# A graph network's head: indices computed ahead of the wait for the floor fill, boundary rows gathered between the scatters

## The reference

```python
src = jnp.concatenate([_s, _d, _loop]); dst = jnp.concatenate([_d, _s, _loop])   # 212,500 edges
_o = jnp.argsort(dst, stable=True); src = src[_o]; dst = dst[_o]                 # sorted by dst
...
def _L0_gnn_ref(x, edge_index, W1, b1, W2, b2):
    x_i = x[dst]
    x_j = x[src]
    edge_features = jnp.concatenate([x_i, x_j - x_i], axis=-1)
    h = jax.nn.relu(edge_features @ W1 + b1)
    edge_messages = h @ W2 + b2
    out = jax.ops.segment_max(edge_messages, dst, num_segments=x.shape[0])
    return jnp.where(jnp.isfinite(out), out, jnp.zeros_like(out))
def _L1_gnn_ref(x, edge_index, edge_attr, u, batch, W1a, ...):
    out = jnp.concatenate([x[row], edge_attr], axis=1)
    out = _mlp(out, W1a, b1a, g1a, be1a, W2a, b2a)      # linear, batch norm, relu, linear
    out = jax.ops.segment_sum(out, col, num_segments=x.shape[0])
    out = jnp.concatenate([x, out], axis=1)
    return _mlp(out, W1b, b1b, g1b, be1b, W2b, b2b)
...
h = jnp.maximum(_layernorm(x, axis=-1), 0.0)
x = x + _L0_gnn_ref(h, edge_index, L0_gnn_W1, L0_gnn_b1, L0_gnn_W2, L0_gnn_b2)
h = jnp.maximum(_layernorm(x, axis=-1), 0.0)
x = x + _L1_gnn_ref(h, edge_index, edge_attr_64, ...)
```

## Time and profile before

| what | value |
|---|---|
| timed, median of 3 runs | 5362.03 us (5359.89 to 5370.35) |
| profiled execution, span from first to last instruction | 5881.6 us |
| POOL busy | 3763.8 us (64%) |
| DVE busy | 2407.0 us (41%) |
| PE busy | 2132.4 us (36%) |
| ACT busy | 1147.2 us (20%) |
| stage 1 | 0 to 343 us |
| stage 2 | 343 to 2677 us |
| stage 3 | 2677 to 2853 us |
| stage 4 | 2853 to 5228 us |
| stages 5 and 6 | 5228 to 5882 us |

### The profile page before, as it was taken

One profiled execution on the slowest core, in us unless ns is written; L12 is line 12 of the kernel. 1 busy time (PEld: TensorE's weight loads), 2 busy tenths in 40 slices (PEclk: granted clock), 3 DMA queues, 4 the chain that ended last, 5 costly groups with the idle time before them and its releaser, 6 DMA issues. The chain is left out here.

```text
span 5881.6 us, 27215 instructions
## 1 busy us (share of the span) xinstructions
PE 2132.4 (36%) x6371; PEld 1168.9 (20%) x6371; DVE 2407.0 (41%) x3005; ACT 1147.2 (20%) x1966; POOL 3763.8 (64%) x3772
## 2 busy tenths in 40 slices
PE   2012222222222222220144344444444344457776
PEld 1001101111010111100022222222222222235555
DVE  5324444444444444446322222222222222259995
ACT  6100000000000000000111111111111111148884
POOL 5667777777777777776666666666666666621112
PEclk9986666566666656665566665666666666668887
DMA  9523323233333333331233333333333333359993
GB/s 352 174 61 82 79 72 80 72 80 75 77 79 73 79 72 80 73 75 38 49 99 88 98 99 88 88 98 88 98 88 99 98 88 98 91 215 423 424 421 124
DMA packets 352728, 710.63 MB, mean 121 GB/s; under 512 B 147428, under 2 KB 219082, under 8 KB 305875
## 3 DMA queue, kind: packets, MB, share of 16 engines
q1 hardware_dynamic: 206708, 573.33, 27.7%
q0 software_dynamic: 119328, 128.91, 11.0%
q10 hardware_dynamic: 26534, 6.66, 0.5%
HBM read 363.85 MB, written 344.74 MB: 120 GB/s over the span
## 5 line engine op out<-in xcount | busy, mean ns | idle before, releaser
L721 POOL DMA_INDIRECT hid<-send_table,node_sums x1664 | 1748.7, 1051 | 554.5 <-issue 554.5
L981 POOL DMA_INDIRECT pairs<-norm_table,node_sums x1664 | 1570.5, 944 | 793.6 <-issue 476.0
L735 PE MATMUL ps_msg<-hidden,w_quarters 128*128 128x512 f32 x832 | 612.3, 904 | 1858.5 <-ACT hidden L748 1171.7
L1001 PE MATMUL ps_hid<-pairs_t,w1a 128*128 128x512 f32 x832 | 684.4, 917 | 1211.5 <-ACT pairs_t L1033 620.3
L1085 DVE TENSOR_SCALAR hid<-ps_hid,vec 128x512 f32<-128x512 f32 x416 | 311.3, 748 | 1743.5 <-DMA mid_row<-recv_table,mid_idx 972.6
L735 PEld LDWEIGHTS ps_msg<-hidden,w_quarters 128*128 128x128 f32 x832 | 237.2, 300 | 2233.0 <-ACT hidden L748 1231.7
L775 DVE STREAM_TRANSPOSE send_t<-hid 128x1024 f32<-128x1024 f32 x104 | 131.0, 1259 | 1274.6 <-DMA hid<-send_table,node_sums 1274.6
L1033 ACT COPY pairs_t<-ps_pairs 128x512 f32<-128x512 f32 x416 | 244.1, 587 | 1721.2 <-remote 1369.2
L748 ACT ACTIVATE hidden<-joined 128x1024 f32<-128x1024 f32 x104 | 109.9, 1056 | 2358.2 <-DMA entries<-dst_groups,group_idx 1236.4
L1218 DVE TENSOR_TENSOR_SCAN total<-ps_mask,total,hid 128x1024 f32<-128x1024 f32 x208 | 488.7, 2350 | 48.7 <-PE ps_mask L1168 26.1
L1001 PEld LDWEIGHTS ps_hid<-pairs_t,w1a 128*128 128x128 f32 x832 | 180.6, 270 | 1296.5 <-ACT pairs_t L1033 661.1
(11 more groups left out here) (163 smaller groups left out, 1949.7 us busy)
## 6 DMA issues: line engine op xcount, KB each, us to landing
hid_edges<-hid SPq DMA_DIRECT2D x104, 1024.0 KB
hid<-hid_edges SPq DMA_DIRECT2D x104, 1024.0 KB
hid_edges<-rows SPq DMA_DIRECT2D x104, 1024.0 KB
recv_edges<-node_sums SPq DMA_DIRECT2D x52, 1024.0 KB
hid<-recv_edges SPq DMA_DIRECT2D x416, 128.0 KB
max_edges<-hid SPq DMA_DIRECT2D x416, 128.0 KB
edge_in<-in_edge_attr_dram SPq DMA_DIRECT2D x415, 128.0 KB
hid<-send_table,node_sums POOLq DMA_INDIRECT x1664
```

What stands on the lines that cost most here:

```text
L721: pool.indirect_dma_start(out=send_in[:, s, j * C:(j + 1) * C], out_offset=None, in_=send_table, in_offset=bass.IndirectOffsetOnAxis(ap=sr ...
L735: mm = nc.tensor.matmul(ps_msg[k % M][:, d, :], w2_quarters[:, b, d, :], hidden[:, s % 2, b, :], start=b == 0, stop=b == BANDS - 1)
L981: pool.indirect_dma_start(out=pairs[:, s, j, 0:C], out_offset=None, in_=norm_table, in_offset=bass.IndirectOffsetOnAxis(ap=src_cols[:, k / ...
L1001: nc.tensor.matmul(ps_hid[s % 2][:, :], w1a[:, :], pairs_t[:, s % 2, :], start=True, stop=True).then_inc(multiplied, 1)
```

## The change

Two things are written in another order, and the boundary rows take another way.

- VectorE's wait for the floor fill, the memset and `mbig` move from before the index chain to behind it, directly ahead of the transposes. Nothing in them is changed.
- POOL's gather of the boundary rows moves from behind the 100 scatters to before pair 44 (`MID_AT`), that is before scatter 88, with its two waits. SP writes the three rows to a DRAM tensor of their own (`mid_rows`) as soon as they are there, and waits for the scatters last.
- Stage 2 begins on SP with six transfers (three quarters, two bands of 32 channels) from `mid_rows` into the last column of `filled[:, 1]`, one element per partition. This column is the start state of the first scan. They wait for VectorE's memsets of it, and VectorE waits for them (`mids_set`) before its first step.

```diff

--- before.py
+++ after.py
@@ -147,6 +147,7 @@
     recv_edges = dram("recv_edges", (EP, C))
     max_edges = dram("max_edges", (EP, C))
     norm_table = dram("norm_table", (NP, C))
+    mid_rows = dram("mid_rows", (3, C))
     CHUNK = 4 * BLK
     assert CHUNK == CO
     hid_edges = dram("hid_edges", (NCO, P, CHUNK))
@@ -305,6 +306,7 @@
 
             pool_passed, dve_passed = sem("pool_passed1"), sem("dve_passed1")
             FILLS = EP * C // (P * CO)
+            MID_AT = NI // 2 - 6
             PIECE_BITS = (P * CO // C).bit_length() - 1
             assert P * CO // C == 1 << PIECE_BITS and NI % 2 == 0
             filled, fill_known = sem("filled"), sem("fill_known")
@@ -359,10 +361,10 @@
                 sp.dma_start(same_max.rearrange("(p c) -> p c", c=CO), mbig[:, :]).then_inc(masks_out, 16)
 
                 sp.wait_ge(mid_gathered, 16)
-                sp.wait_ge(scattered, 16 * NI)
-                sp.dma_start(recv_edges.rearrange("(q e) c -> q e c", q=4)[1:4, 0, :], mid_row[0:3, :]).then_inc(mid_out, 16)
+                sp.dma_start(mid_rows, mid_row[0:3, :]).then_inc(mid_out, 16)
                 sp.wait_ge(mid_out, 16)
                 sp.wait_ge(masks_out, 32)
+                sp.wait_ge(scattered, 16 * NI)
 
             @block.gpsimd
             def _(pool):
@@ -395,6 +397,11 @@
                 pool.wait_ge(fill_known, 1)
                 pool.wait_ge(recv_made, NSTEP)
                 for h in range(NI // 2):
+                    if h == MID_AT:
+                        pool.wait_ge(tables_out, 32)
+                        pool.wait_ge(mid_in, 64)
+                        pool.indirect_dma_start(out=mid_row[:, :], out_offset=None, in_=recv_table,
+                                                in_offset=bass.IndirectOffsetOnAxis(ap=mid_idx[:, 0:1], axis=0)).then_inc(mid_gathered, 16)
                     needed = pool.value_load(fills_needed[0:1, h:h + 1], min_val=1, max_val=FILLS)
                     pool.wait_ge(filled, needed)
                     pool.sem_inc(pool_passed, 1)
@@ -402,10 +409,6 @@
                         pool.indirect_dma_start(out=recv_edges, out_offset=bass.IndirectOffsetOnAxis(ap=start_idx[:, i:i + 1], axis=0),
                                                 in_=recv_sb[:, i, :], in_offset=None,
                                                 bounds_check=EP - 1, oob_is_err=False).then_inc(scattered, 16)
-                pool.wait_ge(tables_out, 32)
-                pool.wait_ge(mid_in, 64)
-                pool.indirect_dma_start(out=mid_row[:, :], out_offset=None, in_=recv_table,
-                                        in_offset=bass.IndirectOffsetOnAxis(ap=mid_idx[:, 0:1], axis=0)).then_inc(mid_gathered, 16)
 
             @block.tensor
             def _(pe):
@@ -581,12 +584,6 @@
                 nc.vector.tensor_tensor(w_ab[:, 0:C], w_ab[:, 0:C], w_ab[:, C:2 * C], ALU.subtract).then_inc(w_made, 1)
 
                 pipeline(dve, SSTEP, SLOTS, [(0, find_group), (3, find_start), (1, norm), (4, add_bias)])
-                for s in range(2):
-                    dve.wait_ge(floor_out[s], 16 * (FILLS // 2))
-                nc.vector.memset(quarter_rows[3 * W:P, E - (P - 1) * IPP:IPP], 0).then_inc(src_padded, 1)
-                dve.wait_ge(masks_made, 1)
-                nc.vector.tensor_scalar(mbig[:, :], m01[:, :], 2 * BIG, -BIG, ALU.mult, ALU.add).then_inc(masks_made, 1)
-
                 def to_row(result, edges, add):
 
                     once.link(nc.vector.tensor_copy(edge_i[:, :], edges))
@@ -631,6 +628,11 @@
                                                              in1=spans[:, :], op0=ALU.is_equal, op1=ALU.mult))
                     once.link(nc.vector.tensor_scalar(spans_mid[:, b, :], spans[:, :], BIG, -BIG, ALU.mult, ALU.add))
 
+                for s in range(2):
+                    dve.wait_ge(floor_out[s], 16 * (FILLS // 2))
+                nc.vector.memset(quarter_rows[3 * W:P, E - (P - 1) * IPP:IPP], 0).then_inc(src_padded, 1)
+                dve.wait_ge(masks_made, 1)
+                nc.vector.tensor_scalar(mbig[:, :], m01[:, :], 2 * BIG, -BIG, ALU.mult, ALU.add).then_inc(masks_made, 1)
                 dve.wait_ge(src_in, 16 * 11)
                 nc.vector.transpose(src_quarters.rearrange("p b a -> p (b a)").bitcast(F32), quarter_rows[:, :].bitcast(F32)).then_inc(src_made, 1)
                 for k in range(KH):
@@ -668,7 +670,7 @@
             (recv_turned, send_turned, fill_done, join_done, hidden_done, msg_done, max_done, rows_made, w2_clear, w2_in) = (
                 sem(n) for n in ("recv_turned", "send_turned", "fill_done", "join_done", "hidden_done", "msg_done", "max_done",
                                  "rows_made", "w2_clear", "w2_in"))
-            fill_start = sem("fill_start")
+            fill_start, mids_set = sem("fill_start"), sem("mids_set")
             block = s2.enter_context(nc.Block())
 
             def by_row(tile):
@@ -684,6 +686,12 @@
                 recv_v = recv_edges.rearrange("(q k p j) c -> q k p (j c)", q=4, p=W, j=JQ)
                 max_v = max_edges.rearrange("(q k p j) c -> q k p (j c)", q=4, p=W, j=JQ)
                 mask_v = same_max.rearrange("(q k c) -> q k c", q=4, c=BLK)
+                sp.wait_ge(fill_start, 2 * BANDS)
+                with nc.allow_non_contiguous_dma(reason="one element per partition"):
+                    for q in range(1, 4):
+                        for b in range(BANDS):
+                            sp.dma_start(filled[q * W:(q + 1) * W, 1, b, BLK - 1:BLK],
+                                         mid_rows[q - 1:q, b * W:(b + 1) * W].rearrange("a p -> p a")).then_inc(mids_set, 16)
                 sp.wait_ge(w2_clear, 1)
                 for q in range(4):
                     for b in range(BANDS):
@@ -755,6 +763,7 @@
                     nc.vector.memset(filled[:, 1, b, BLK - 1:BLK], -BIG).then_inc(fill_start, 1)
                     nc.vector.memset(maxima[:, 1, b, BLK - 1:BLK], -BIG).then_inc(fill_start, 1)
                 dve.wait_ge(fill_start, 2 * BANDS)
+                dve.wait_ge(mids_set, 16 * 3 * BANDS)
 
                 def fill(r, s):
                     k = r * U + s
```

## The result

The changed kernel takes **5334.12 us** (median of 4 runs, 5332.78 to 5335.07); the kernel before, on the same chip, takes 5360.96 (4 runs, 5359.58 to 5370.35). The ratio is 0.9948 with a 95% interval of 0.9935 to 0.9962: 26.8 us or 0.52% faster.

A forecast was written before the change was run, and what follows sets the result against it. POOL's indirect gathers were taken to bound the long stages 2 and 4. Terms: −1.2 (chain starts earlier) + 0.2 (POOL) + 0 (boundary rows) + 0 (added transfers) = −1.0 us, giving 5361.0 us, range 5346 to 5369.

The forecast's parts named there:

- the price of the wait: Stage 1, VectorE before the index chain: fill complete 1.4 us before VectorE needs it, so the wait costs nothing.
- Rival A: Head: in timed runs VectorE is ahead of the floor fill, old kernel loses 13.6 us there; 5347.4 us, chance 0.18.
- The two moved instructions: Head: memset and mbig leave the index chain's path, 1.2 us gained, less 0.2 for POOL running beside them.
- The boundary rows: End of stage 1: SyncE about 1.2 us earlier in the barrier, but POOL's drain closes the stage; gain 0.
- Rival B: End of stage 1: POOL's drain is short without the profiler, so SyncE's 1.2 us count too; 5359.8 us, chance 0.10.
- The added transfers: Start of stage 2: six transfers take 2.5 us of SyncE's issue, but POOL does not wait; cost 0.
- Source loads and the tables: Stage 1: later source loads have 80 us of cover, the boundary gather's tables 57 us; cost 0.
- rival C: Start of stage 2: new transfers bring POOL's slow pace on at once, ten steps by 2.4 us; 5385 us, chance 0.06.
- D: Head: POOL blocked for both moved instructions (1.16 us), or the receive table holds the scatters; stays 5362.0 us, chance 0.06.

The follow-up runs named there:

- new profile of before: The kernel before, unchanged, profiled a second time: 5360.36 us, with a span of 5358.6.
- the two runs that part them from the wait: Whole change with only the wait put back ahead of the index chain: 5359.26 us; whole change with memset and mbig back there, without the wait: 5334.08 us.
- the memset behind them: The whole change with a 128x128 memset on POOL behind the last scatter: 5334.99 us, ratio 0.995 to the kernel before.
- faster version: The whole change with the first 20 columns' indices computed inside the norm loop and scattered early, boundary gather before pair 47: 5319.12 us, ratio 0.9921.

## Why the prediction was wrong, and where it was right

**The step that failed: the price of the wait.** The prediction read a margin of 1.4 us for the fill out of the first profile, and said that in this execution the wait costs nothing. Of that execution this was true. The failure is in the step that carried it over to the timed runs: "So I take the head to be about as long in the timed runs". The timed median stood 519.6 us below that span. The prediction placed 491 of it in POOL's gathers, which was right (496 by the new profile), and treated the other 29 as too little to matter. But a surplus of 28 us in VectorE's head is all that it takes to turn a wait of 26.3 us into one of zero. The new profile of before shows it: receive table at 157.85 in place of 186.03, the fill at about 184 in both. The runs put that wait, 26.3 us long, in the place of the zero: the wait's move alone gave the whole gain, and the wait put back took it away.

**The sum as it was.** First scatter: 191.46 − 164.56 = 26.9 us earlier. Start of stage 2: 331.44 − 305.05 = 26.4 us earlier. Timed: 26.8. Of this the two moved instructions are 0.75 to 0.83 by the two runs that part them from the wait, and the wait is the rest, about 25.6.

**Rival A was right in kind and too small.** Its mechanism is the one that decided: VectorE is ahead of the fill in the timed runs. Its size came from spreading the surplus evenly, 8.8% of 169 us or 15 us, and the surplus was not even: 28 us. With 28 in place of 15, a number that only the later profile gives, its own working gives 28 − 1.4 = 26.6 us for the wait and 1.0 for the rest, 5334.4 us, against 5334.12 measured. Its chance, 0.18, was set too low by an argument that doesn't hold: "DVE's stalls fall together with POOL's gathers, which are real work". The gathers stand beside the same VectorE steps in the new profiles, without these stalls: of the ten L211 in the new profile of before, nine run wholly inside a gather, and none has idle time ahead of it. So the stalls were part of the stretched execution. A surplus that shows beside real work is not thereby real itself.

The Trainium skill (SBUF — State Buffer, section "SBUF: two separate sides") gives the lock of the shared ports a condition that the prediction left out: a VectorE operation with two SBUF inputs takes it only against a GpSimd operation that reads SBUF. The prediction let the stall of the earlier trace rows agree with the lock. The new profile of before takes that agreement away: the same operation on two inputs starts at 54.54, in the midst of the gather of 54.30 to 55.25, and does not wait. So these gathers don't block it. What stalled it in the first profile stays open.

**The two moved instructions.** Predicted 1.2 less 0.2 for POOL, 1.0 in all. In the changed kernel the scatter beside `mbig` (189.44) lasts 1.16 us in place of 0.98, which is the 0.2. For the whole the traces give 0.75 and 0.83. That bears the term out to within the spread from profile to profile: the receive table alone was done at times up to 1.1 us apart in the nine later ones. No timing shows it.

**The boundary rows.** Predicted 0, since POOL's drain closes the stage. Borne out: the boundary rows alone measure 1.0001, with SyncE 2.4 us earlier in the barrier (1.2 were predicted) and the drain's end unmoved. In the changed kernel the drain ends 9.1 us after POOL's last transfer, as in the earlier trace rows (9.2). The reason given, that the drain belongs to POOL's transfers, is not shown: with the memset behind them, its end kept its distance from the memset. The forecast needs only that POOL's last instruction stays where it was, and it did (321.18 against 321.25). Rival B, a drain that is short in timed runs, would have made this kernel some 2.4 us faster; the timing alone doesn't exclude that, since its interval reaches down to 0.9992, 4.3 us. What speaks against B is that the later profiles, whose spans agree with the timed runs, have the drain's end 9.1 to 9.2 us behind POOL's last instruction.

**The added transfers.** Predicted 2.5 us on SyncE and 0 on the path. They took 2.63 us, and the first join still waited 5.20 us for gathers. With five times as many, the weights 11.2 us later and the first join 5.8 us later, the time was the same. Borne out.

**Source loads and the tables.** The transposes end at 241.6 + 3.4 = 245.0, and POOL scatters until 294.9: about 50 us of cover where 80 were predicted, since the scatters themselves moved. The tables of the boundary gather are out by 262.2 and the gather comes at 278.41: 16 us of cover where 57 were predicted. POOL waited for neither (0.30 us ahead of the gather, as ahead of any scatter), as predicted, but both margins shrink by the gain itself: the earlier the scatters start, the less of them is left. The faster version puts the gather ahead of pair 47 for this reason.

**Rivals C and D.** Stage 2 keeps 20.0 us a step, in the changed kernel and in the new profile of before; no later profile has the slow pace of 22.4 us, and so rival C loses its ground. What tipped the pace in the first profile stays open. The two halves of D fall with the first scatter 26.9 us earlier and with the one scatter that grew by 0.2 us and not by 1.16.

**What is given back.** The fill ends 4.4 us later when scatters run beside its last parts (memset at 188.55 against 184.16; 190.25 in the faster version). It costs nothing here, since what waits for it has the cover named above: about 50 us for the source indices, 16 us for the tables, whose transfers wait for the fill too.

## What to carry to other kernels

Before a margin of one or two microseconds is read out of a profile, compare its span with the timed median. Here they differed by a tenth, and the difference wasn't spread evenly. A first sum found nearly all of it, and the little that was left was enough to hide the wait. In such a case every wait whose two sides are of different kinds, instructions on one and transfers on the other, should be priced with the whole unplaced rest on either side, or the profile taken again.

Work that needs nothing from a wait belongs ahead of it even where the wait looks empty in one profile. What then comes later is the work that stood behind the wait, so look up its cover first (here 50 us were left). With that cover the move is an insurance against the runs in which the wait is not empty.

After a wait is gone, look at once at the idle time ahead of the same instruction: here POOL's 15.05 us were still there, and a second cut of the same chain brought 15 us more.

## What the runs showed of the hardware

One profiled execution of the kernel before had a span of 5881.6 us, where the next one had 5358.6 and the timed runs about 5361. Of the surplus 226 us lay in stage 2's gathers (2303.2 against 2077.3 for the same 1664, of which 178 us in the gathers' own busy time, 1748.7 against 1570.5) and 270 us in stage 4's (2347.5 against 2077.1, and there the busy time was the same, 1570.5 and 1570.4). VectorE's head was 28 us longer. Of these 28 the first scatter shows only 1.9 (193.38 against 191.46), since in the shorter execution VectorE waits instead; the floor fill ended at about 184 in both. Pauses among the scatters brought the start of stage 2 to 11.7 us later (343.11 against 331.44). The cause of the surplus stayed open; it did not come back in the nine later profiles, so no run could try it.

POOL's drain before the barrier of stage 1 ended 9.1 to 9.2 us after POOL's last instruction in all ten profiles, whether that was a scatter, a gather or the memset. At the next three barriers the distance was another: in the new profile of before the drain ended 5.3, 8.3 and 6.7 us after the last gather of stages 2, 3 and 4. Before the barrier of stage 5, where all of its transfers have landed, the drain lasted the same in the old and in the new kernel, to the nanosecond that the record gives (the old one stands in the earlier trace rows; this is the new one):

```profile
L1113 POOLq DRAIN  x1: 8232/8232/8232, 5235.5 to 5235.5; - x1
```
